# A graph network with attention and mixture layers on one core: GpSimd pauses before every fourth gather of the second edge stage instead of every third

## The reference, cut to what matters

```python
xg0 = y0[edge_src]; xg1 = y1[edge_src]          # one row of 256 values for each edge
h = silu(edge_scalars @ fc_w1 / sqrt(8)) * 1.679
w = h @ fc_w2 / 8                                # four 64-wide weights for each edge
mid0 = w_a * xg0 * ea0
mid1 = w_b * einsum('euc,ec->eu', xg1, ea1) / sqrt(3)
mid2 = (w_c * xg0)[:, :, None] * ea1[:, None, :]
mid3 = (w_d * ea0)[:, :, None] * xg1
agg = segment_sum(concatenate([mid0, mid1, mid2, mid3]), edge_dst)
```

## Time and profile before

| | |
|---|---|
| Median of 3 runs | 3897.82 us (3890.13 to 3904.57) |
| Profiled execution, its own time | 3894.28 us |
| Span of its records | 3892.4 us |
| PE busy | 3077.4 us, 79% |
| DVE busy | 2265.2 us, 58% |
| POOL busy | 1897.1 us, 49% |
| ACT busy | 1431.5 us, 37% |
| Mean granted TensorE clock | 0.88 |

### The profile page before, as it was taken

How to read it: one execution, slowest core, us unless ns; L and a number is a source line. 1 busy time by engine, 2 the same in 40 slices (tenths; PEclk the granted TensorE clock), 3 DMA queues, 4 the chain that set the end, 5 groups by cost and what they waited for, 6 DMA issues and landing times. The chain is left out here.

```text
span 3892.4 us, 80642 instructions
## 1 busy us (share of the span) xinstructions
PE 3077.4 (79%) x22728; PEld 2325.2 (60%) x22728; DVE 2265.2 (58%) x6165; ACT 1431.5 (37%) x4367; POOL 1897.1 (49%) x2266
## 2 busy tenths in 40 slices
PE   6477777777777768879997887888888888888499
PEld 4366666665666656658885544555554554557488
DVE  5455555555555556757665655666666666666712
ACT  5122222222222213732332544455454544416422
POOL 3556566656666652101112656656655566541154
PEclk9788788878888879989997989998999988889799
DMA  6433333333333334743322333333333333325321
GB/s 196 124 85 89 85 88 85 88 83 88 88 88 87 88 97 123 199 112 90 89 82 86 90 88 90 91 90 89 90 89 87 90 90 90 94 79 160 116 53 48
DMA packets 239107, 375.93 MB, mean 97 GB/s; under 512 B 88190, under 2 KB 145606, under 8 KB 238762
## 3 DMA queue, kind: packets, MB, share of 16 engines
q0 software_dynamic: 89712, 230.26, 21.5%
q1 hardware_dynamic: 147482, 140.83, 12.9%
q10 hardware_dynamic: 1696, 2.62, 0.2%
HBM read 310.75 MB, written 62.84 MB: 96 GB/s over the span
## 5 line engine op out<-in xcount | busy, mean ns | idle before, releaser
L586 POOL DMA_INDIRECT e_rows<-tab,e_ix x830 | 794.0, 957 | 539.6 <-issue 253.3
L1984 POOL DMA_INDIRECT e_rows<-tab,e_ix x828 | 787.8, 951 | 432.4 <-issue 342.3
L981 PE MATMUL e_pU<-e_ohp,e_rows 128*128 128x128 f32 x3340 | 527.4, 320 | 74.7 <-issue 70.4
L981 PEld LDWEIGHTS e_pU<-e_ohp,e_rows 128*128 128x128 f32 x3340 | 501.6, 235 | 85.6 <-issue 79.0
L2226 PE MATMUL e_pU<-e_msg,e_oh 128*32 128x128 f32 (+1 forms) x6672 | 425.4, 324 | 57.9 <-issue 47.4
L695 ACT CAST e_ohT<-e_pT 64x640 bf16<-64x640 f32 x167 | 114.6, 686 | 886.4 <-remote 472.1
L2156 DVE TENSOR_TENSOR e_msg<-e_pW,e_rows 128x256 f32<-128x256 f32 x417 | 176.6, 423 | 450.9 <-remote 250.7
L2158 DVE TENSOR_TENSOR e_msg<-e_pW,e_rows 128x384 f32<-128x384 f32 x834 | 422.2, 548 | 0.0
L2212 PE MATMUL e_pW<-e_w,e_hT 64*128 64x256 f32 x1668 | 332.6, 449 | 75.1 <-DVE e_oh L2142 23.5
L2226 PEld LDWEIGHTS e_pU<-e_msg,e_oh 128*32 128x32 f32 x6672 | 262.9, 117 | 208.5 <-issue 151.4
L962 PE MATMUL e_pT<-ident,e_oh 128*64 128x128 f32 x835 | 149.7, 319 | 206.1 <-DVE e_oh L487 134.8
(11 more groups left out here) (453 smaller groups left out, 5696.4 us busy)
## 6 DMA issues: line engine op xcount, KB each, us to landing
e_rows<-tab,e_ix POOLq DMA_INDIRECT x1658
xnT<-f_xnT SPq DMA_DIRECT2D x25, 250.0 KB, 3.1
e_xk<-xnT SPq DMA_DIRECT2D x25, 250.0 KB
xnT<-b_xT SPq DMA_DIRECT2D x25, 250.0 KB, 2.9
m_xnT<-xnT SPq DMA_DIRECT2D x25, 250.0 KB
xnT<-m_xT SPq DMA_DIRECT2D x25, 250.0 KB, 2.7
ffn_norm<-xnT SPq DMA_DIRECT2D x25, 250.0 KB
tab<-f_hrow SPq DMA_DIRECT2D x25, 227.5 KB
```

Source lines behind the costliest of these rows:

```text
L586: nc.gpsimd.indirect_dma_start(out=rows[:, s, j, :], out_offset=None, in_=env["tab0"], in_offset=bass.IndirectOffsetOnAxis(ap=at[:, j:j + ...
L981: nc.tensor.matmul(pU[:, s % 2, 2 * W * k:2 * W * (k + 1)], rows[:, s, j, 128 * k:128 * k + 128], ohp[:, s % 3, j, 2 * k:2 * k + 2, :], st ...
L1984: nc.gpsimd.indirect_dma_start(out=rows[:, r % PER, j, :], out_offset=None, in_=env["tab1"], in_offset=bass.IndirectOffsetOnAxis(ap=at[:, ...
```

## The change

On GpSimd alone, in the second edge stage, the places of the rests and of the index copy move. Two groups (twelve gathers) now have three rests, at places 0, 4 and 8: before gathers 0 and 4 of a group with even `r`, and before gather 2 of one with odd `r`. Each still waits for the gather issued two before. The index copy stands before gather 2, and so do the waits for gathers 2 to 5 of the previous group. The gathers, their data and the other engines' code stay as they are.

```diff
                         for j in range(T1):
-                            if lo >= 1:
-                                for i in ((j,) if j < 3 else range(3, T1) if j == 3 else ()):
+                            if j == 2:
+                                for i in range(2, T1) if lo >= 1 else ():
                                     hold(pool, s_row[i], 16 * g)
-                            if j == 3:
-                                hold(pool, s_row[1], 16 * (g + 1))
-                            elif j == 0 and lo >= 1:
+                                if hi <= GROUPS1 - 2:
+                                    nc.gpsimd.tensor_copy(ix[:, (r + 1) % 2, :], srcI[:, bass.ds((g + 1) * T1, T1)])\
+                                      .then_inc(s_ix, 1)
+                            elif j < 2 and lo >= 1:
+                                hold(pool, s_row[j], 16 * g)
+                            if r % 2 == 0 and j == 4 or r % 2 == 1 and j == 2:
+                                hold(pool, s_row[j - 2], 16 * (g + 1))
+                            elif r % 2 == 0 and j == 0 and lo >= 1:
                                 hold(pool, s_row[T1 - 2], 16 * g)
-                            if j == 3 and hi <= GROUPS1 - 2:
-                                nc.gpsimd.tensor_copy(ix[:, (r + 1) % 2, :], srcI[:, bass.ds((g + 1) * T1, T1)])\
-                                  .then_inc(s_ix, 1)
```

## The result

The changed kernel takes 4104.46 us (median of 6 runs, 4094.06 to 4114.50), the kernel before 3897.69 (6 runs, 3890.13 to 3908.25): a ratio of 1.0533 [1.0510, 1.0556], 207 us slower. The forecast was 3906, in a range of 3845 to 3952.

What follows compares the result with a forecast made beforehand. It took GpSimd's consumers, with PE slowed by gather runs, to bound the second edge stage. To 3894.3 it added +11 and +5 for early groups, 0 for 109 groups, -2 and -2 at the end: 3906 us, range 3845 to 3952.

Steps and rivals of the forecast that it cites:

- The reading of the kernel before: Second edge stage: consumers at 10.14 us a group set the pace, GpSimd 3.7 groups ahead; gather runs slow PE, pauses free it.
- GpSimd's own saving: Second edge stage: fewer rests save GpSimd 0.54 us a group, all hidden while its consumers are slower.
- What longer runs cost the consumers: Second edge stage: runs of four instead of three cost consumers +0.45 us a group, bounds -0.3 and +1.0.
- What the lead does to it: Second edge stage: buffers fill after some 25 groups, then runs average three and the cost returns to 10.14, +-0.2 us a group.
- rival C: Second edge stage: runs of four cost 0.45 us in every group, +62 us, 3956 us; chance 0.15.
- over 10.5 us: Sign in the second edge stage: a consumer group over 10.5 us after 2500 us would prove rival C.
- A: Rival, second edge stage: GpSimd's pace counts after all, 138 groups gain 0.54 us, -75, 3820 us; chance 0.13.
- B: Rival, second edge stage: waiting for a full buffer rests PE better than the rests, -18 to -30, some 3870 us; chance 0.19.
- D: Rival: the change does nothing, PE's stops follow the number of gathers alone, 3894 us; chance 0.45 together with the forecast.

Runs made afterwards that it cites:

- e8: The changed kernel, unaltered, against the kernel before, on a free chip: 3486.41 us, ratio 0.9810.
- e2: The kernel before with the changed kernel's rests alone, the index copy left before gather 3, on a free chip: 3478.36 us, ratio 0.9799.
- e6: The kernel before with a rest in front of every second gather, index copy where it was, on a held chip: 4013.44 us, ratio 1.0313.
- e3: The kernel before with rests before gathers 0 and 4 of every group (runs of four and two), on a free chip: 3552.65 us, ratio 1.0011.
- e5: The kernel before with no rests in the second edge stage, on a free chip: 3343.31 us, ratio 0.9412.
- e7: Against the kernel before: gathers left out after the fifth group, later groups reuse the rows, on a free chip: 3354.87 us, ratio 0.9442.
- e11: The kernel before with no rests in the second edge stage, on a held chip: 4368.00 us, ratio 1.1228.
- e13: The kernel before, rests kept, each gather bringing 64 columns of a row instead of 256, on a free chip: 3469.20 us, ratio 0.9755.
- e14: The kernel before with 64-column gathers and no rests in the second edge stage, on a free chip: 3343.89 us, ratio 0.9410.
- e15: Against the kernel before: gathers left out after the fifth group, run again, on another free chip: 3357.10 us, ratio 0.9440.
- e10: The kernel before with GpSimd at most three groups ahead instead of five, on a held chip: 3897.03 us, ratio 1.0010.

## Why the prediction was wrong

**The reading of the kernel before was right**, for the chip it was made on: a lead of 3.7 groups, consumers at 10.14 us, PE breaking off in runs of gathers and going on in the pauses. On free chips GpSimd paces it (removing the rests gains 211 us), which the one profile couldn't tell.

**GpSimd's own saving was right.** 0.54 us a group was worked out from the rests. On free chips, where it reaches the end, 138 x 0.54 = 75 us was due and 68 came (e8), 71 with the copy left in place (e2).

**The step that failed is "What longer runs cost the consumers".** It said +0.45 us a group, +1.0 at most; the first groups, 2120 to 2220 us, show +3.9 and the steady stretch +1.44. I had worked it out from idle shares: from the first stage's 0.44 us a gather against 0.27 here, linearly from runs of three to runs of six. That averages a stage with another order of work, and it treats a stop as time lost in proportion to the gathers. What a stop costs is what comes late behind it: VectorE's unexplained waits rose from 2.0 to 3.0 us a group, and in the first groups from 14.0 / 10.3 = 1.4 to 44.1 / 7.3 = 6.0. There one such wait grew from 2.8 to 3.7 us in the mean, no more than the 1.25 us that I gave for one gather; but there were 12 in 7.3 groups and not 5 in 10.3 (waits, 2120 to 2220 us). The sum had no term for stops that come more often. The granted clock falls as well: 0.78 over 2100 to 2300 us against 0.87, 0.87 against 0.91 later. One matmul of the dense layer took 684 ns before and 772 after (groups by line, 2300 to 3300 us, of before and of after):

```profile
L2249 PE MATMUL e_pKV<-e_wkv,ffn_norm 128*125 128x512 f32 x316 | 175.5, 684 | 0.0
```
```profile
L2251 PE MATMUL e_pKV<-e_wkv,ffn_norm 128*125 128x512 f32 x276 | 175.8, 772 | 0.0
```

**"What the lead does to it" failed next.** The runs came as I said: of the changed kernel's runs from 2300 to 3000 us 61 are of four and 53 of two (counted in the timeline), three in the mean. But that was to bring back the cost of now, 10.14 +-0.2, and it is 11.58. So the mean length of the runs doesn't set the cost; I had left myself 0.2 us for the curve, and it was 1.4. e6 can't say what a run of two costs, since its 10.83 is GpSimd's own pace, and runs of four and two in every group (e3) were not made on a held chip. The slack before gather 0 that I worked out as 1.5 us and set against rival C was there (3.39 us in the group shown), but it didn't bring the old cost back.

**The rivals.** C comes nearest to what happened on the held chips: its mark "over 10.5 us" is met. Its own condition, a slack of under 1.0 us at gather 0, is not, so it is right in its outcome and not in its reason; its price, 0.45 x 138 = 62 us, had the same error as mine, and was 199. That the clock would go down with it was noted there and not priced. A is what happens on free chips, to within 7 us. B and D are out on both. That chips differ was no rival of mine, and the same change has one sign on one kind of chip and the other on the other.

**The two rules that the prediction named.** The Trainium skill (SBUF — State Buffer, "SBUF: two separate sides") says that engine ports and DMA ports never contend. On free chips e5 and e7 agree with it (all gathers or hardly any, 0.941 and 0.944). On a held one PE stood in each run of e11; whether ports have a part in that no run tells. The Trainium skill's advice to issue a DMA early and wait for it late (DMA: Bandwidth & Descriptors, "Rules for kernel authors") is what leaving out the rests comes to, and that gave 0.941 on free chips and 1.123 on the held one.

**Open.** What holds PE on a held chip: the bytes of the gathers, their issuing by GpSimd, or something that both share. e13 and e14 would tell it there, but ran on free chips, as e15 did: the consumers' own pace on a held chip is unmeasured too. Neither alone fits plainly, since in e11 PE stood for 5.4 us after the last gather was issued and 3.5 us after data had ceased to move. That longer runs cost more on a held chip rests on the first run of e11, the first groups, and e10 against P; how much of the cost is the stop and how much the clock that falls with it isn't separated, nor what the copy's new place adds there. Why chips differ isn't known.

A version that beats both kernels everywhere wasn't found. Without rests it is 0.941 on free chips and the worst of all on a held one; the rests of before are the best tried on held chips.

## What to carry to other kernels

A tuned pause that protects one engine from another has a best place, and a straight line through averages of another stage won't give its slope: before removing such a pause, bound the loss by what is late if the protected engine stops for the whole run. Where a kernel's margin is against contention, measure on more than one chip; the sign of a change can turn on which chip it runs on. And read a stage's first groups, before buffers fill: they show a cost bare that later waits cover in part.

## What the runs showed of the hardware

- Two kinds of chip. The kernel before takes 3549 to 3559 us (medians) on five chips and 3896 us on a sixth (3898 where the prediction was made), with no value between. Most of the difference lies in the first edge stage: 736 gathers and copies in 1000 us are 8.15 us a group of five gathers and a copy; 755 in 800 us on a free chip are 6.36. Times 167 groups that is some 300 of the 343 us (an estimate). The window there, of e8:

```profile
300.00:1100.00 800.00, 650.56 (x5520) 573.99 (x5519) 589.91 (x1634) 271.68 (x462) 622.84 (x755) 0.92 0.42 112
```

- On a held chip a long run of gathers issued by GpSimd all but stops TensorE: 15 matmuls in 34 us, with the granted clock at 0.55, where the same code makes 340 at 1.00 on a free one; and TensorE goes on in full only 3.5 us after the last data have moved (e11, e5).
- On free chips the gathers cost the stage nothing that could be measured: without rests it is 0.9412 at 108 GB/s, 0.9410 at 36, and 0.9442 with the gathers left out after the fifth group.
- Waiting before every gather for the one two before it makes pairs, 3.49 us for two, not an even spacing.
